# Products that nobody reads, in 55 places where TensorE stands idle, in a hybrid attention, FFN and state-space block

## The reference

```python
x = x + attn(layernorm(x), Wq, Wk, Wv, Wo)    # 16 heads of 8; a window of 32 and every 64th key, causal
x = x + ffn(layernorm(x), k0, k1, k2, s0, s1, s2)
x = x + mamba(layernorm(x), ...)              # a scan over time with 256 channels x 16 states
x = x + ffn(layernorm(x), k0, k1, k2, s0, s1, s2)
```

## Time and profile before

| | us |
|---|---|
| median of three runs | 879.61 (879.34 to 879.76) |
| the profiled execution, its own time | 871.1 |
| its span, first to last instruction | 869.2 |
| PE busy | 702.7 (81%), 6624 matmul records |
| DVE busy | 732.1 (84%) |
| ACT busy | 604.6 (70%) |
| POOL busy | 664.4 (76%) |
| mean granted clock of TensorE | 0.923 of 2.4 GHz |

### The profile page before, as it was taken

One profiled execution on the slowest core, in us unless ns is written; L12 is line 12 of the kernel. 1 busy time (PEld: TensorE's weight loads), 2 busy tenths in 40 slices (PEclk: granted clock), 3 DMA queues, 4 the chain that ended last, 5 costly groups with the idle time before them and its releaser, 6 DMA issues. The chain is left out here.

```text
span 869.2 us, 19741 instructions
## 1 busy us (share of the span) xinstructions
PE 702.7 (81%) x6624; PEld 407.7 (47%) x6624; DVE 732.1 (84%) x1226; ACT 604.6 (70%) x1152; POOL 664.4 (76%) x818
## 2 busy tenths in 40 slices
PE   4788977997877989998999789878986866865557
PEld 2765644654535446654546345346542442422133
DVE  6996327998999899998979999999999986899941
ACT  5766588788786888778769886875667647554412
POOL 5133427878899979788998689889899998898740
PEclk9999989998999899998999999999997978887678
DMA  5000019787958889484977799798688996999900
GB/s 185 2 3 2 1 41 239 185 221 204 246 138 225 191 228 257 127 192 125 239 211 195 196 261 240 181 242 228 155 217 220 270 244 158 250 276 250 253 1 24
DMA packets 83879, 154.73 MB, mean 178 GB/s; under 512 B 9402, under 2 KB 9795, under 8 KB 83779
## 3 DMA queue, kind: packets, MB, share of 16 engines
q1 hardware_dynamic: 83778, 153.48, 67.7%
HBM read 142.43 MB, written 11.01 MB: 177 GB/s over the span
## 5 line engine op out<-in xcount | busy, mean ns | idle before, releaser
L1545 POOL TENSOR_TENSOR d<-d,cr 128x1024 f32<-128x1024 f32 x128 | 302.0, 2361 | 28.8 <-DVE d L1090 19.2
L1351 ACT ACTIVATE ps<-dt,An 128x512 f32<-128x512 f32 x256 | 174.6, 691 | 81.2 <-DVE d L1090 80.7
L1090 DVE TENSOR_TENSOR_SCAN d<-ps,hl,d 128x512 f32<-128x512 f32 x128 | 160.1, 1268 | 8.2 <-ACT ps L1351 2.9
L1090 DVE TENSOR_TENSOR_SCAN d<-ps,d 128x512 f32<-128x512 f32 x128 | 152.7, 1211 | 10.3 <-ACT ps L1351 3.4
L751 PE MATMUL ps<-h,w 128*128 128x512 f16 x512 | 123.2, 389 | 10.2 <-DVE h L1037 6.5
L1078 DVE TENSOR_TENSOR d<-ps,d 128x512 f32<-128x512 f32 x184 | 122.1, 670 | 1.0 <-DMA d<-dud 0.8
L687 PE MATMUL ps<-KD,qm 128*128 128x128 f32 (+1 forms) x512 | 106.7, 342 | 0.9 <-DVE qm L950 0.9
L820 PE MATMUL ps<-d,cst 128*32 128x512 f32 x512 | 75.0, 661 | 24.4 <-POOL d L1545 24.3
L1533 POOL TENSOR_TENSOR d<-d,br 128x512 f32<-128x512 f32 x72 | 91.5, 1273 | 4.2 <-DMA d<-dud 4.1
L687 PEld LDWEIGHTS ps<-KD,qm 128*128 128x128 f32 x512 | 86.1, 200 | 11.7 <-issue 1.3
L751 PEld LDWEIGHTS ps<-h,w 128*128 128x128 f16 x512 | 48.3, 100 | 84.7 <-DVE h L1037 22.2
(11 more groups left out here) (146 smaller groups left out, 1278.3 us busy)
## 6 DMA issues: line engine op xcount, KB each, us to landing
dt<-dtd SPq DMA_DIRECT2D x256, 256.0 KB, 4.8
d<-dud SPq DMA_DIRECT2D x256, 256.0 KB, 5.0
dtd<-sR SPq DMA_DIRECT2D x16, 256.0 KB, 2.6
dud<-sE SPq DMA_DIRECT2D x16, 256.0 KB, 3.6
X<-in_x SPq DMA_DIRECT2D x8, 256.0 KB, 6.8
br<-bcd SPq DMA_DIRECT2D x8, 256.0 KB, 3.3
cr<-bcd SPq DMA_DIRECT2D x8, 256.0 KB, 3.7
out<-X SPq DMA_DIRECT2D x4, 512.0 KB, 4.4
```

The costliest lines, as they stand in the source:

```text
L1090: eng.tensor_tensor_scan(d, banks[u % NG][:, :], d, hl[:, r:r + 1] if m % 2 else 0.0, ALU.mult, ALU.add).then_inc(v_sc, 1)
L1351: eng.activation(banks[u % NG][:, :], DT[:, u % NT, :], ACT.Exp, scale=An[:, g:g + 1]).then_inc(s_da, 1)
L1545: eng.tensor_tensor(d, d, CR[m % 2][:, :].unsqueeze(1).to_broadcast((128, 2, 512)), ALU.mult).then_inc(p_cm, 2)
```

## The change

A table `WARM` is added with 55 entries (place, bank, number of products), and a step `warm_t` for TensorE. The entries are sorted into the timetable with the others; each stands right ahead of the step that has the same place number. Such a step waits until the bank is emptied by its last user's reader and until the identity is loaded, then multiplies the identity by itself, a 128 x 128 x 128 product in f32, `products` times into the same 128 columns. It takes no turn in the ring, signals no semaphore, and nothing reads what it writes. In all there are 376 products, from 1 to 27 in a place. All other steps and their order are the same.

```diff
+WARM = [
+    (952, 2, 8), (1038, 2, 5), (2055, 2, 3), (3760, 4, 5), (7804, 4, 2), (7928, 4, 2), (12616, 5, 11), (12772, 7, 3), (13473, 7,
...
+    (75010, 5, 16), (75155, 5, 1), (77016, 5, 2), (77769, 5, 6), (78045, 4, 6), (78858, 4, 27), (79674, 4, 27), (80075, 4, 11),
+    (81206, 5, 3), (81823, 5, 3), (82152, 5, 8), (82854, 5, 18), (83068, 5, 5), (84155, 5, 2),
+]
...
-    rows = []
+    rows = [(at, "warm_t", (k, products)) for at, k, products in WARM]
...
+            def warm_t(k, products):
+                for s, v in emptied.get(k, ()):
+                    eng.wait_ge(s, v)
+                eng.wait_ge(l_w1, 16)
+                for _ in range(products):
+                    eng.matmul(banks[k][:, 0:128], ident, ident, start=True, stop=True)
```

More of the change, by code:

```diff
@@ L834, in mout_t @@
                 t.then_inc(t_mo, 1)
-            mine = {"aln_t": aln_t, "aqk_t": aqk_t, "aval_t": aval_t, "asc_t": asc_t, "atr_t": atr_t, "apv_t": apv_t,
+            def warm_t(k, products):
[4 more added lines that the diff above has]
+                    eng.matmul(banks[k][:, 0:128], ident, ident, start=True, stop=True)
+            mine = {"warm_t": warm_t, "aln_t": aln_t, "aqk_t": aqk_t, "aval_t": aval_t, "asc_t": asc_t, "atr_t": atr_t, "apv_t": apv_t,
                     "jout_t": jout_t, "fln_t": fln_t, "fl1_t": fl1_t, "fl2_t": fl2_t, "fl3_t": fl3_t,
```

## The result

The changed kernel takes **857.18 us** (median, 855.76 to 858.3), the kernel before 879.48 beside it: ratio 0.975, 95% interval 0.973 to 0.978, so 22.3 us less. Forecast were 8.2 us less, 871.4, in a range from 865 to 878. The direction was right, the size was not. The profiled execution went from 871.1 to 858.1 us, span 869.2 to 856.2: 13.0 us less. So of the 22.3 us only 13 show between the two traces, and both differences have to be explained.

The account below looks back on a forecast made before the run. DVE, busy 84% of the span, was taken as leading, with TensorE binding only the serial end. Minus 3.8, minus 6.4, 0 and plus 2.0 took the profiled 871.1 to 863; plus 8.5 gave 871.4 us, range 865 to 878.

Parts of the forecast that it names:

- the carry-over from the profiled execution to the median: Whole run: the median shown lies 8.5 us above the profiled execution, and this difference stays the same after the change.
- Term 1, the end: Serial chain of the last 37.2 us: output product, transposes and last FFN pass run at full clock, minus 3.8 us.
- Term 2, the middle: 150 to 832 us: DVE waits caused by PE's low clock shrink, between 0 and 12.7 us; half taken, minus 6.4.
- Term 3, the start: First transposes and key copy: earlier clock rise against five products without idle time; 0 taken, ends minus 0.8 and plus 2.3.
- Term 4, the losses: 13 products at 253 us waiting for bank 7, plus fillers longer than their gaps: 0 to 5.4 us, plus 2.0 taken.
- The overruns at the late column sums: 27 products (6.4 us) in 5.14 us of idle time before the sum at 803.30: 1.3 us late, within 3.7 overall.
- The clock: Whole span: fillers keep TensorE's granted clock up, so its mean goes from 0.923 to 0.97 or more.
- a fall repairs itself through the fillers: At any gap: a low-clock filler takes twice as long, fills its gap and brings the rise within a filler or two.
- fillers at the low clock: Rival: products don't hold the clock up and cost 0.469 us each, 5.3 us on the end's chain: 884.9; chance 0.09.
- gains absorbed: Rival: POOL and transfers take the middle's whole gain and losses reach 5.4 us: 881, or 879; chance 0.10.
- half the effect: Rival: the clock stays low in about half of its low stretches, gain some 4 us: 875.6; chance 0.12.
- all low time coming back: Rival: the kernel is bound by PE wherever the clock is low, 67 us gained, 812; chance 0.01.

Follow-up runs that it names:

- experiment 5: Changed kernel with only the five table entries from 77769 to 80075 (77 products, late column sums, 790 to 820 us): 878.45 us, ratio 1.001 to the kernel before.
- Experiment 9: Changed kernel with only the first six table entries (25 products, up to 81 us): 877.48 us, ratio 1.000 to the kernel before.
- experiment 1: Changed kernel with only the last six table entries (the serial chain of the last 40 us): 875.41 us, ratio 0.997 to the kernel before.
- experiment 2: Changed kernel with only the 43 table entries from 12616 to 80075 (120 to 820 us): 860.56 us, ratio 0.981 to the kernel before.
- experiment 10: Changed kernel with only the 16 table entries from 12616 to 31558 (80 products, 122 to 322 us): 869.15 us, ratio 0.991 to the kernel before.
- 11: Changed kernel with only the 22 table entries from 40367 to 77016 (155 products, 405 to 785 us): 869.36 us, ratio 0.991 to the kernel before.
- experiment 8: Changed kernel with 15 places enlarged or new, one bank moved, the 5 products at 1038 removed, 18 inside one layer 2 (445 products): 853.46 us, ratio 0.973.
- experiment 12: Changed kernel without the 5 products at 1038 (between the first two groups of transposes): 857.03 us, ratio 0.977 to the kernel before.
- experiment 3: Changed kernel with all 376 products cut from 128 moving columns to 8: 900.58 us, ratio 1.025 to the kernel before.

## Why the prediction was wrong, point by point

The forecast of 871.4 us was 14.2 us too high. It was made of two parts: 863 for the profiled execution, where 858.1 was measured (4.8 us off), and 8.5 us from there to the median, where minus 0.9 was measured (9.4 off).

**The step that failed most is the carry-over from the profiled execution to the median**: "that difference is carried over as it is". The 8.5 us between them were taken for something fixed, and they were not. Profiling as such doesn't shorten a run: in the changed kernel and the twelve experiments the profiled run lies between 4.0 us below and 3.8 above the median of its kernel. The one of before, 871.1 us, is shorter than all 44 runs of the kernel before that stood beside the experiments (871.5 to 883.3), and its mean clock, 0.923, is the highest among theirs (0.906 to 0.923, median 0.912). A straight line through the 44 falls 5.7 us for 0.01 of clock, which would make 0.011 some 6 us of the 8.5. That is a correlation and not a price: experiment 5 raised the mean clock by 0.013 and gained nothing. What counts is where the low stretches fall.

The traces show it directly. Experiment 9 has fillers up to 81 us alone and the same median as the kernel before (ratio 1.000), yet its trace is 5.3 us longer than the trace of before (span 874.5 against 869.2), and by the table above most of it comes between 211 and 714 us, where the two kernels are the same. The trace of experiment 5, also without a gain in the median, is 6.3 us longer. So the profiled execution was a run in which low stretches happened to miss some costly places; it was luck, which a median doesn't have. One such place is the first FFN pass, which ran at full clock in the trace of before (layer 1 in 1.89 us). Five experiments have no filler there (1, 2, 5, 10, 11), and in all five profiles a low stretch meets this pass. In that of experiment 5, PE and DVE show:

```profile
81.98 3.38 PE L744 MATMUL ps<-h,w 128*128 128x512 f16 x8 [0.77 <-issue]
...
85.82 7.07 PE L754 MATMUL ps<-h,w 128*128 128x512 f16 x32
```

```profile
94.05 0.69 DVE L982 TENSOR_REDUCE mn<-ps 128x8 f32<-128x512 f32 x1 [7.34 <-PE ps L690]
```

Layer 1 takes 3.38 us instead of 1.89, and DVE is 2.0 us later than before at the scores behind it, of which 0.7 stood there already ahead of the pass; in the five profiles the pass costs DVE 0.8 to 2.5 us. The changed kernel's trace has three low stretches left in place of 20, its runs lie together, and its profiled run (858.1) is near its median. The gain over a typical run is therefore larger than the gain over that trace: 22.3 against 13.0. This may also be why experiment 10 gave 8.7 us by the medians where its own trace, against that of before, wins 6.6 between 121 and 324 us.

**Term 1, the end, was right.** The parts were forecast as 1.85, 0.45 and 1.51 us; DVE's starts show 1.72, 0.47 and 1.45, together 3.6, the trace of experiment 1 shows 3.6 as well, and its medians give 3.1.

**Term 2, the middle, was too small even for the trace.** It was half of a bound of 12.7 us: minus 6.4. Between 120 and 776 us the two traces differ by 10.2, after losses. "Whatever DVE gains may be spent in its next wait for POOL or for a transfer" happened in part: the products L1078 of 300.26 and 749.21 (times of before) wait 1.61 and 1.55 us for a transfer in the changed kernel where they waited 0.13 and 0.28, and 1.5 and 1.3 us are given back. Two other losses are of another kind. 1.5 us between 395 and 409 and 1.3 at 776 us lie at low stretches that the changed kernel itself still has (396.6 to 403.4 and 761.8 to 768.6 us); at the second DVE waits 3.03 us for a column sum that takes 1.94. In the trace of experiment 8, which has no low stretch there, DVE gives back nothing in these two places. So half was too small a share of the bound, and the bound was too low as well, since its largest item was under-sized: from 714 to 732.06 us DVE wins 4.5 us, and I priced only L800, 1.1 us. In the changed kernel:

```profile
716.60 2.05 PE L854 MATMUL ps<-cst 128*128 128x128 f32 x16
...
719.01 1.88 PE L811 MATMUL ps<-u,wgt 128*41 128x512 f32 x4 [0.36 <-ACT u L1327]
...
721.95 0.75 DVE L1117 SCALAR_TENSOR_TENSOR u<-u,wgt,ps 128x512 f32<-128x512 f32 x1 [3.19 <-PE ps L831]
```

DVE's wait falls from 6.21 to 3.19 us. The products ahead of L800 had run in a low stretch as well (707.6 to 717.8 us), L780 above all, before and changed:

```profile
712.85 3.78 PE L780 MATMUL ps<-xnT,w 128*128 128x512 f32 x4 [0.93 <-ACT xnT L1286]
```

```profile
706.82 1.98 PE L791 MATMUL ps<-xnT,w 128*128 128x512 f32 x4 [0.26 <-ACT xnT L1306]
```

That is 1.8 us, and the first of the products L790 behind them give 0.7 more. So ACT's `u`, its table load and everything behind it came sooner, and so did the column sum that PE does after L800 (1.06 us instead of 1.58). The wait's last releaser is not its whole price: what stands in front of the releaser in its engine's order counts too.

**Term 3, the start:** I took 0 with ends of minus 0.8 and plus 2.3; it was plus 1.04 in the trace.

```profile
5.63 2.77 PE L854 MATMUL ps<-cst 128*128 128x128 f32 x12
...
11.02 2.34 PE L854 MATMUL ps<-cst 128*128 128x128 f32 x10
...
15.27 2.79 DVE L948 COPY KD<-ps 32x512 f32<-32x512 f32 x4 [3.42 <-PE ps L644]
```

The five products ran at the low clock's speed, 2.34 us, just as the upper end had it, though the granted clock reads 1.00 there, as it does for the start in the trace of before. The first eight did not bring the clock up before 12.2 us; the copy of L948 starts at 15.27 instead of 14.22. The delay stays on DVE until 121 us, and in the trace of experiment 12, which leaves the five products out, it is missing there and at the end. The medians don't resolve it (experiments 9 and 12).

**Term 4, the losses, was 2.0 us and should have been about nothing.** The filler of 13 products does not wait for ACT's copy of the keys:

```profile
246.38 0.45 PE L722 MATMUL ps<-v,pt 128*32 128x18 f32 x32
246.76 3.17 PE L854 MATMUL ps<-cst 128*128 128x128 f32 x26
250.40 1.90 PE L752 MATMUL ps<-h,w 128*128 128x512 f16 x8 [0.47 <-DVE h L1052]
```

It starts right behind L722, and layer 1 follows 0.47 us behind its end. I had read the wrong bank: `aqk_t` takes two, and bank 7 holds the queries, whose copy by ACT is over at 246.60 in this trace; the copy of the earlier trace rows, which is called a reader of bank 7 there, is of the keys and reads the other bank. The overruns at the late column sums are harmless too:

```profile
786.91 1.06 PE L831 MATMUL ps<-d,cst 128*32 128x512 f32 x8 [0.52 <-POOL d L1565]
787.90 6.29 PE L854 MATMUL ps<-cst 128*128 128x128 f32 x54
794.13 1.06 PE L831 MATMUL ps<-d,cst 128*32 128x512 f32 x8
795.12 6.29 PE L854 MATMUL ps<-cst 128*128 128x128 f32 x54
802.67 1.06 PE L831 MATMUL ps<-d,cst 128*32 128x512 f32 x8 [1.25 <-POOL d L1565]
```

27 products take 6.29 us, the first sum starts as soon as they end, and DVE's difference stays at minus 9.3 throughout. Experiment 5 says that these cost nothing by the medians. The other overruns were not tested by themselves, but for the one at the start (term 3).

**The clock** stayed up, as forecast (0.990, more than 0.97): its trace has three low stretches of 3 to 7 us. That a fall repairs itself through the fillers is not shown. Two of the three hold no filler at all, and 11 of the 20 low stretches of the trace of before, without any filler, are as short as the shortest of them (3.4 us). **Rivals:** fillers at the low clock occurred in two places only (the 13 products at the start, and eight at 581 us) and were made in experiment 3; gains absorbed fell with experiment 2; half the effect fell with the 22.3 us; all low time coming back fell with them and with experiment 5, where 27 us of low time went and 0 was gained. The rule of the Trainium skill (TensorE: Matmul & The Clock Gate, Terms), time at the low clock x (1 - K/N), makes an estimate of 13 to 14 us for experiment 5 and of 67 us for the whole kernel by the trace of before, three times what came; the measurements decide.

## What to carry to other kernels

Before a forecast is made against one trace, ask how that execution lies among the others: where the granted clock falls by chance, the profiled run may be the lucky one, and a change that makes the clock steady can gain more on the median than against the trace. In this kernel a low clock cost time only where somebody waited for TensorE, directly or through one more engine: look for waits of the busiest engine that end with PE, and count the slow work ahead of the releaser as well. Where a gain is lost again, look whether the changed kernel has a low stretch of its own left there. Filling idle gaps with dense products somewhat shorter than the gaps (here 89 us of them, by the prediction's count, in 121 us of idle time) paid in this kernel; the same fillers made thin or twice as long cost more than they bring.

## What the runs showed of the hardware that was not expected

Products of 8 columns between full weight loads kept PE busy (37.19 of 37.5 us) while the granted clock stayed at its lower level, and the mean clock of that kernel was 0.905 to 0.912; with 128 columns it was 0.990 to 0.992, with f32 transposes of 128 columns 0.964 to 0.974. A thin product is not cheaper than a full one: worked out from the traces of experiment 3 and of the changed kernel, the median distance from one filler record to the next (two to a product) is 112 ns at the full level and 213 at the low one in both. And the kernel before spreads by 1.3% over its 44 runs on three chips (871.5 to 883.3), and by 0.9 to 1.1% on each, with a longer time at a lower mean clock; the changed kernel spreads by 0.3% and the version of experiment 8 by 0.2%, over four runs each.
